# Recurrent block, one core: VectorE takes the maxima ahead of the copies in odd steps and behind them in even ones, with the reciprocal between maxima and bias

## The reference, cut to what matters

```python
qkv = x @ Wqkv
q, k, v = split heads (16 heads of 64)
q = l2norm(q) * qs ; k = l2norm(k) * ksc
q = q * cos * scale + rotate_half(q) * sin * scale
k = k * cos / scale + rotate_half(k) * sin / scale
sim = einsum('bhwie,bhwje->bhwij', q, k) * 8.0
sim = where(outside the window of 32 back, -max, sim)
attn = softmax(sim, -1)
out = einsum('bhwij,bhwje->bhwie', attn, v) @ Wo
```

## Time and profile before

| | us |
|---|---|
| median of 3 runs | 3623.99 (3622.72 to 3632.03) |
| the profiled execution, its own time | 3630.74 |
| its span, first to last instruction | 3628.9 |
| PE busy | 3309.8 (91%) |
| DVE busy | 3210.5 (88%) |
| ACT busy | 3014.5 (83%) |
| POOL busy | 2883.4 (79%) |

### The profile page before, as it was taken

The page is one execution under the profiler, slowest core; times in us unless marked ns, Lnnn a source line. Parts: engine busy times, 40 slices in busy tenths (PEclk is TensorE's granted clock), DMA queues, the critical chain, the costliest instruction groups (busy, mean ns, idle before and its releaser), DMA issues.

```text
span 3628.9 us, 92884 instructions
## 1 busy us (share of the span) xinstructions
PE 3309.8 (91%) x29710; PEld 2117.3 (58%) x29710; DVE 3210.5 (88%) x11256; ACT 3014.5 (83%) x8812; POOL 2883.4 (79%) x2383
## 2 busy tenths in 40 slices
PE   7887899999999999999999999999999989999998
PEld 3444556656556656656556566666656556656655
DVE  7998988988988988988988888898888888888986
ACT  6554888888888888888888888888888888888887
POOL 6887877888887888877888887888887788887883
PEclk9998999999999999999999999999999999999999
DMA  5443323333323333322333322333322333332322
GB/s 160 140 133 123 110 100 101 103 113 109 112 100 101 106 115 107 115 100 99 105 115 106 114 102 98 108 115 105 117 100 99 105 115 104 112 105 98 105 102 91
DMA packets 261729, 396.24 MB, mean 109 GB/s; under 512 B 45566, under 2 KB 86588, under 8 KB 261244
## 3 DMA queue, kind: packets, MB, share of 16 engines
q1 hardware_dynamic: 261244, 390.30, 32.0%
HBM read 157.91 MB, written 6.03 MB: 45 GB/s over the span
## 4 chain that ended last, share of the span: by engine, by line
PE 40%; DVE 27%; ACT 17%; issue 11%; POOL 4%; DMA 1%; DVEq 0%; SPq 0%; ACTq 0%; POOLq 0%
DVE ab L1603 8%; PE bank L879 8%; ACT pr L1177 7%; DVE sm L1651 7%; PE bank L868 6%; PE bank L839 5%; PE bank L907 4%; PE bank L355 3%; DVE pt L1638 3%; DVE wide L1495 3%; PE bank L357 3%; PE bank L356 3%; PE bank L824 2%; ACT sq L1165 2%; PE bank L849 2%
## 5 line engine op out<-in xcount | busy, mean ns | idle before, releaser
L1177 ACT ACTIVATE pr<-sm,nb,rq 128x128 f32<-128x128 f32 (+1 forms) x3072 | 1520.9, 503 | 160.5 <-DVE nb L1657 159.2
L1338 POOL TENSOR_TENSOR pr<-pr,rden 128x640 f32<-128x640 f32 x768 | 964.3, 1256 | 487.3 <-DVE rden L1628 487.3
L1603 DVE TENSOR_TENSOR ab<-bank,ltab 128x512 f32<-128x512 f32 x1520 | 974.9, 683 | 44.4 <-PE bank L357 35.2
L1352 POOL TENSOR_TENSOR rot<-ab,swp 128x512 f32<-128x512 f32 x760 | 975.8, 1284 | 39.4 <-DMA swp<-ab 31.1
L1651 DVE CUSTOM_DVE_ANT_0 sm<-bank,mask 128x128 f32<-128x128 f32 (+1 forms) x3072 | 753.5, 301 | 4.8 <-PE bank L839 4.7
L1638 DVE COPY pt<-bank 128x512 f32<-128x512 f32 x768 | 525.3, 684 | 96.0 <-PE bank L850 88.7
L1177 ACT ACTIVATION_READ_ACCUMULATOR pr<-sm,nb,rq 128x1 f32 x3072 | 601.7, 196 | 0.0
L1358 POOL TENSOR_TENSOR rot<-rot,rkb 128x512 f32<-128x512 f32 x384 | 491.1, 1285 | 83.1 <-DMA rkb<-k_scratch 82.9
L1165 ACT ACTIVATE sq<-bank 128x512 f32<-128x512 f32 x768 | 455.2, 593 | 86.3 <-DVE ab L1603 78.6
L868 PE MATMUL bank<-pt,vtok 128*64 128x160 f32 (+1 forms) x6144 | 461.1, 292 | 42.5 <-ACT vtok L1191 40.4
L839 PE MATMUL bank<-rot 64*64 64x96 f32 (+1 forms) x12288 | 342.9, 243 | 96.9 <-DVE nb L1657 81.6
(11 more groups left out here) (213 smaller groups left out, 5713.9 us busy)
## 6 DMA issues: line engine op xcount, KB each, us to landing
swp<-ab SPq DMA_DIRECT2D x1520, 128.0 KB, 2.0
rkb<-k_scratch SPq DMA_DIRECT2D x768, 128.0 KB, 2.9
rot<-c_scratch SPq DMA_DIRECT2D x64, 256.0 KB, 3.4
sq<-c_scratch SPq DMA_DIRECT2D x64, 256.0 KB, 3.3
xs<-xT SPq DMA_DIRECT2D x95, 128.0 KB, 2.3
xs<-xT SPq DMA_DIRECT2D x95, 127.5 KB, 2.4
raw<-Wqkv SPq DMA_DIRECT2D x48, 128.0 KB, 2.6
wo<-Wo SPq DMA_DIRECT2D x6, 512.0 KB, 5.1
```

Source lines behind the costliest of these rows:

```text
L1177: ins = act.activation(pr[:, s % 4, i, t, 0:P + WINDOW * t], sm[:, s % 2, i, cs], ACT.Exp, bias=nb[:, s, t, i:i + 1], scale=head_scale(rq, ...
L1338: ins = pool.tensor_tensor(pr[:, e % 4, :, :, :], pr[:, e % 4, :, :, :], rden[:, e, :, :].rearrange("p t i -> p i t").unsqueeze(3) .to_bro ...
L1352: pool.tensor_tensor(rot[:, PAIRS * (j % 2) + j // 2, :], ab_of(j, 0, lead), swp_of(j, lead), ALU.add).then_inc(qk_rot, 1)
L1603: ins = dve.tensor_tensor(seqs(ab_of(j, i, lead)), seqs(qk_bank(j, lead)[:, :]), ltab[:, 2 * (j % 2) + i:2 * (j % 2) + i + 1, :] .to_broad ...
```

## The change

`maxima` loses its last part, which becomes a function `bias(s)`, and the calls in the loop of VectorE are put in another order. In odd steps it is now maxima, reciprocal, bias, copy, products; in even steps transpose and copy, maxima, reciprocal, bias, products. What stood behind the products (`scale_q`, `gated`, `clamp`) still does, and `residual` and `products(15)` still stand ahead of the products, now behind the bias. No instruction is added or removed. The wait on `sc_max`, ahead of the bias, stays.

```diff
                     ins.then_inc(sc_max, 1)
+
+                def bias(s):
+
+                    p, b = s // 2, s % 2
                     dve.wait_ge(sc_max, n16 + (s + 1))
...
+                    if s % 2 and cur is not None:
+                        maxima(s)
+                    if s % 2 == 0 and s < 4 and prev is not None:
+                        copy_probs(s + 12, prev)
+                    if s % 2 == 0 and s >= 4 and cur is not None:
+                        copy_probs(s - 4, cur)
+                    if s % 2 == 0 and cur is not None:
+                        maxima(s)
                     if s < 2 and prev is not None:
                         denominators(s + 14, prev)
                     if s >= 2 and cur is not None:
                         denominators(s - 2, cur)
-                    if s < 4 and prev is not None:
+                    if cur is not None:
+                        bias(s)
+                    if s % 2 and s < 4 and prev is not None:
                         copy_probs(s + 12, prev)
-                    if s >= 4 and cur is not None:
+                    if s % 2 and s >= 4 and cur is not None:
                         copy_probs(s - 4, cur)
...
                         clamp(0, nxt)
-                    if cur is not None:
-                        maxima(s)
```

## The result

| | before | after |
|---|---|---|
| median of 4 runs, us | 3624.76 (3622.72 to 3632.03) | 3896.21 (3893.54 to 3901.60) |
| span of the profiled execution | 3628.9 | 3899.8 |
| granted TensorE clock over the span | 0.995 | 0.981 |

The changed kernel takes 1.0747 times as long (95% interval 1.0728 to 1.0766), 271 us more, where 159 us more were forecast. The sign was right; the time lies 46 us above the upper end of the range.

A forecast was written before the change was run, and what follows sets the result against it. The bound was taken to change from step to step among PE, DVE and ACT. Terms 1.11 + 0.70 + 1.51 = 3.32 us a turn, times 48, add 159 us: 3790, less 6.75 gives 3783 us; range 3600 to 3850.

The forecast's parts named there:

- The three terms: Added time in stretches 14 to 0, 0 to 2 and 6 to 8: 1.11 + 0.70 + 1.51 = 3.32 us a turn.
- +0.70 for 0 to 2: Steps 0 to 2: projection 0 waits for square 15, behind later products, starting at 3.97 instead of 3.27: 0.70 us a turn.
- +1.51 for 6 to 8: Steps 6 to 8: the later copy delays transposes 7 from 4.23 to 5.74; stretch 7.72 instead of 6.21 us.
- 1.11: Steps 14 to 0: square 13 starts 3.32 instead of 2.21 us after the scores, passed on in full through ACT.
- 12 to 14 stays: 0: Stretch 12 to 14 keeps its 8.36 us, since POOL's scale_k waits for a reciprocal at 4.18 instead of 4.20 us.
- before scores 12 the loop of 7.1 us takes it: Before scores 12, the gain from the ended bias wait is taken by the loop of 7.1 us; counted 0.
- the cover of 7.1 us: Stretches where PE's own work is longer hide the 7.1 us loop without a residual; others lose what they lie under 7.1.
- Waits given back: 0: PE's waits for late biases before scores end, 0.99 us in the turn; counted 0, with 81.6 us in all as upper end.
- The bias and POOL: Bias behind the reciprocal goes in before POOL; counted 0, bounds: 218 us vanish, or 504 holds of about 1 us.
- Rival 1: PE's waits for biases were the bound, so PE runs ahead: 3542 us, down to 3520; chance of faster 0.16.
- Rival 2: No change: gains in 8 to 14 meet losses elsewhere, or square 13's delay is made up: 3624 us; chance 0.07.
- Rival 3: Much slower: the reciprocal lets POOL in ahead of the bias, 504 holds of 1 us, half on the path: 4035; chance 0.05.

## Why the prediction was wrong in size, by its own steps

**The three terms** held. +0.70 for 0 to 2 measured +0.78, +1.51 for 6 to 8 measured +1.48. The second match is in part luck: in a clean turn the stretch went from 6.21 to 7.73 us as worked out, but before the change its mean is 6.70, and after it 8.18, with 6 of the 36 turns at 9.84 that have the clock at half in this stretch. For 14 to 0 the path was right, down to the square at 3.38 and the stretch of 12.42, but the term of **1.11 was mis-sized**: it was taken from a turn of 11.26, and the kernel before does that stretch in 10.92 on average, since it has turns like the second one. No turn after is under 12.41, and 23 of the 36 stand at 12.41 or 12.42, so the true term is 1.49, 18 us more over 48 turns. The text had priced this (14 us) and put it in the range instead of in the sum. The other 0.40 us a turn came with the clock at half.

**"12 to 14 stays: 0" and "before scores 12 the loop of 7.1 us takes it", counted 0,** is the step that failed: 1.17 and 0.77 us a turn, 93 us of the 126 by which 285 exceeds the forecast's 159. The two waits that were priced in 6 to 8 and in 0 to 2 came once more, in the stretches held to be covered. In 10 to 12 PE stood 1.71 us a turn before transposes for the copy (0.12 before); the wait for a bias that this replaced, before scores 12, had been 0.74. In 12 to 14 it stood 0.74 us before a projection for a square (0.12 before), although the text ahead of the prediction says that steps 11 to 15 share bank 5 as steps 0 to 3 do. Why the cover of 7.1 us did not hold: first, the prediction followed what waits for DVE's moved instructions but not what the moved instructions wait for. Maxima 11 ask for exponentials 9 before these are done, 0.68 us in the turn shown of the changed kernel; a third buffer ended that. Second, of the products' users it priced ACT's square and left out SP (the swaps, and `rkb` behind them), and of the reciprocal's it took only the start in step 13, not POOL's list behind the late one of step 10. The loop of 7.1 us knew only DVE and PE. How the 0.77 us of 12 to 14 divide between the square, the copy, POOL and the clock stays open.

**"Waits given back: 0"** came out near. The 81.6 us are gone, but only 8 to 10 became shorter, by 0.16 us a turn; elsewhere other waits stand in their place, as in 10 to 12. With the odd steps alone, where the same waits are gone, the time is 20 us lower.

**The bias and POOL, "I count 0".** The order of starts was read rightly (the bias follows 0.12 us behind the reciprocal, where 0.09 was worked out, and POOL 0.25), but its consequence wasn't drawn: holds do not stay as they are, they halve, from 218 to 103 us, and undoing the reciprocal alone costs 87 us. Without this gain the miss would have been larger.

**Rival 1** (faster) fell where the text said that it would be decided: maxima 14 wait 2.05 us for the scores in the turn shown, so the scores don't run ahead:

```profile
1868.00 0.29 DVE L1651 CUSTOM_DVE_ANT_0 sm<-bank,mask 128x128 f32<-128x128 f32 x1 [2.05 <-PE bank L839]
```

**Rival 2** (no change) fell since square 13's delay wasn't made up by anything. **Rival 3** fell with the group of the bias. What neither the forecast nor a rival had is the clock.

## What to carry to other kernels

When an instruction is moved to an earlier place in an in-order list, list what *it* waits for (buffers in use, above all), and when one is moved to a later place, follow all its users, a DMA queue's next entries among them, until somebody has slack. When a wait has been priced at one place, look for the same wait in every other step of the loop. Price a stretch by its mean over all rounds, not by the round that is at hand. An order need not be the same in all steps: the odd half of this change, with one more buffer where its maxima waited, is 1.1% faster than the kernel before, while the even half costs 7.5%, and one step of 16 makes 87 us of it by itself and 121 in the changed kernel.

## What the runs showed of the hardware

**TensorE's clock fell in turns with idle stretches.** In the changed kernel PE stands idle between 3.3 and 6.6 us after scores 14: 0.7 us before the projection that waits for square 13, and 1.61 us before the feed-forward's first matmul, which waits for a gelu. In 13 of the 36 middle turns the stretch from 14 to 0 is then longer than 12.6 us. In each of these 13, and in none of the other 23, the granted clock is at half for a part of the stretch, 1.2 GHz instead of 2.4. Two windows of one of them, before and during:

```profile
2459.07:2465.00 5.93, 4.26 (x58) 2.95 (x58) 4.99 (x25) 3.34 (x8) 5.00 (x5) 1.00 0.25 91
2465.20:2471.70 6.50, 6.03 (x19) 3.27 (x20) 1.94 (x4) 5.31 (x13) 3.38 (x3) 0.50 0.21 81
```

and its first matmul there, which took 0.51 us in the turn shown further up:

```profile
2465.67 0.79 PE L355 MATMUL bank<-xn_h,w_h 128*128 128x512 f32 x1 [1.61 <-ACT gg L1217]
```

The stretch from 14 to 0 became 14.72 us instead of 12.42. From 400 us to the end of the turns, the trace of before has nothing at half clock; that of the changed kernel has 102 us in 28 pieces, that of the reciprocal alone 601 us in 123, and that of the new order in step 14 alone 72 us in 20. In the mean of 14 to 0 this is 0.40 us a turn, 19 us of the time. It is in other stretches too: 6 to 8 took 9.84 us in the 6 turns that have half clock there and 7.84 in the others, 10 to 12 took 10.12 in 3 turns and 8.53 in the others. That would be 22 us more, an upper bound, since other things differ in those turns. Idle time that a wait opens on PE can so cost more than itself; which idle stretch brings the clock down and which doesn't stays open, since turns with the same waits went both ways.

**A wait with a semaphore from DVE** reaches POOL later than DVE reaches its own next instruction: 0.25 against 0.12 us behind the same reciprocal. A bias put right behind the reciprocal was in first and was hardly held in even steps, 6 us in all against 109 with the reciprocal first. It doesn't help where POOL is already at work: the biases of odd steps in the changed kernel still cost 97 us, and in all but one of the 243 that took over 0.25 us POOL was then in an instruction other than the normalisation.
